# Expert loop of a routed vision tower: the second expert's gate and up projections moved one tile ahead, the row transposes moved to the end of the step

## The reference, cut to what matters

```
macro_scores = sigmoid(xf @ macro_w)                 # T x 4: one group of the four is chosen
micro_scores = sigmoid(einsum('td,gde->tge', xf, micro_w))
w = (macro_full[:, :, None] * micro_full).reshape(T, 8)
gate = silu(einsum('td,edf->tef', xf, gate_w))       # 256 -> 512
up = einsum('td,edf->tef', xf, up_w)                 # 256 -> 512
h = gate * up
out = einsum('te,tef,efd->td', w, h, down_w)         # 512 -> 256
```

## Time and profile before

| | |
|---|---|
| median of 3 runs | 2495.08 us (2494.74 to 2496.54) |
| the profiled execution | 2493.25 us, of which the profile's span is 2491.4 us |
| busy share of the span | PE 89%, DVE 74%, ACT 65%, POOL 47% |
| the expert loop | from 2288.3 us to the end of the span, about 203 us |

### The profile page before, as it was taken

One profiled execution on the slowest core, in us unless ns is written; L12 is line 12 of the kernel. 1 busy time (PEld: TensorE's weight loads), 2 busy tenths in 40 slices (PEclk: granted clock), 3 DMA queues, 4 the chain that ended last, 5 costly groups with the idle time before them and its releaser, 6 DMA issues.

```text
span 2491.4 us, 61244 instructions
## 1 busy us (share of the span) xinstructions
PE 2223.1 (89%) x19318; PEld 1660.7 (67%) x19318; DVE 1833.0 (74%) x5685; ACT 1607.2 (65%) x4899; POOL 1175.8 (47%) x2201
## 2 busy tenths in 40 slices
PE   0289999999989999999989999999899999988998
PEld 0257777777767777777667777777677777765655
DVE  8667777777767787777767777777678888886533
ACT  3257777776667777776667777777677777774322
POOL 1046555554556555555555555554566555541101
PEclk9889999999999999999999999999999999999999
DMA  3564444445554444444644444445543334345110
GB/s 118 140 172 116 106 107 112 113 129 155 132 158 123 111 109 111 106 123 144 180 118 114 113 110 113 121 135 146 158 106 97 94 100 109 99 136 187 54 46 23
DMA packets 378059, 295.35 MB, mean 119 GB/s; under 512 B 45087, under 2 KB 350721, under 8 KB 376739
## 3 DMA queue, kind: packets, MB, share of 16 engines
q1 hardware_dynamic: 370603, 272.41, 41.8%
q10 hardware_dynamic: 4864, 12.68, 1.5%
q0 software_dynamic: 2272, 6.35, 0.7%
HBM read 137.45 MB, written 72.07 MB: 84 GB/s over the span
## 4 chain that ended last, share of the span: by engine, by line
PE 33%; ACT 24%; DVE 12%; POOL 8%; SPq 7%; issue 6%; DMA 4%; DVEq 0%; POOLq 0%; ACTq 0%
ACT e_rows L2168 11%; PE bk L2066 5%; PE bk L2078 5%; SPq L1532 4%; PE bk L1272 4%; ACT p_flat L2150 4%; PE bk L2035 4%; PE bk L1906 3%; DVE x L2425 3%; DVE o_rows L2333 3%; ACT rel L2099 2%; POOL arena L1727 2%; PE bk L1894 2%; POOL arena L1725 2%; PE bk L1845 2%
## 5 line engine op out<-in xcount | busy, mean ns | idle before, releaser
L2168 ACT ACTIVATE e_rows<-e_rows,nb 128x257 f32<-128x257 f32 x1024 | 516.1, 515 | 34.9 <-DVE nb L2362 34.2
L2362 DVE CUSTOM_DVE_ANT_0 e_rows<-bk,arena 128x257 f32<-128x257 f32 x1024 | 390.1, 418 | 72.0 <-PE bk L1940 70.7
L1845 PE MATMUL bk<-hin,arena 128*128 128x257 f16 x3072 | 422.0, 274 | 16.7 <-DMA hin<-hd_dram 11.1
L2324 DVE TENSOR_TENSOR p_flat<-bk,p_flat 128x512 f16<-128x512 f32 x512 | 353.8, 691 | 66.7 <-ACT p_flat L2150 54.2
L1894 PE MATMUL bk<-ident,e_rows 128*128 128x128 f32 x2048 | 324.9, 281 | 51.8 <-ACT e_rows L2168 29.3
L1727 POOL TENSOR_TENSOR arena<-rel,arena 128x257 f16<-128x257 f32 x496 | 328.3, 662 | 41.4
L1845 PEld LDWEIGHTS bk<-hin,arena 128*128 128x128 f16 x3072 | 296.4, 97 | 67.4 <-issue 18.6
L1725 POOL TENSOR_SCALAR arena<-rel 128x257 f16<-128x257 f32 x496 | 203.7, 411 | 265.1 <-ACT rel L2099 258.4
L2150 ACT ACTIVATE p_flat<-bk 128x512 f16<-128x512 f32 x512 | 310.0, 605 | 7.9 <-PE bk L1894 7.9
L1894 PEld LDWEIGHTS bk<-ident,e_rows 128*128 128x128 f32 x2048 | 222.4, 141 | 136.9 <-ACT e_rows L2168 115.3
L1775 POOL TENSOR_SCALAR wf<-wf 128x256 f32<-128x256 f32 x216 | 94.1, 436 | 363.9 <-DMA wf<-in_w_dram 187.7
(11 more groups left out here) (327 smaller groups left out, 4232.8 us busy)
## 6 DMA issues: line engine op xcount, KB each, us to landing
arena<-arena SPq DMA_DIRECT2D x768, 128.5 KB, 3.5
wf<-in_w_dram SPq DMA_DIRECT2D x168, 128.0 KB, 2.8
w_split_dram<-wh SPq DMA_DIRECT2D x168, 128.0 KB, 2.4
xs_dram<-in_c_blank_dram SPq DMA_DIRECT2D x24, 772.5 KB
wf<-in_we_dram SPq DMA_DIRECT2D x96, 128.0 KB, 2.6
we_split_dram<-wh SPq DMA_DIRECT2D x96, 128.0 KB, 1.9
w_rest<-w_split_dram SPq DMA_DIRECT2D x12, 1024.0 KB, 17.2
arena<-we_split_dram SPq DMA_DIRECT2D x8, 1536.0 KB, 12.0
```

Of the source, the lines that this page charges most:

```text
L1845: r_ = mm(bank[4 + s % 2][:, 0:S], wcol(a, C_QKV, k, 3 * HD, chunk_at(s)), hin[:, m, k, :], start=i == 0, stop=i == 5)
L2168: act.activation(E[:, h % EB, qt, :], E[:, h % EB, qt, :], ACT.Exp, bias=nb[:, 2 * h + qt:2 * h + qt + 1], scale=-1.0, accum_out=sums[:, q ...
L2324: v.tensor_tensor(pt[:, h, 1, :, 0:IMG], bank[2 + h % 2][:, :].rearrange("p (k s) -> p k s", k=QT), pt[:, h, 0, :, 0:IMG], ALU.subtract).t ...
L2362: v.tensor_tensor_reduce(E[:, h % EB, qt, :], bank[qt][:, 0:S], cb[:, h, :], -SCORE, 3e38, ALU.add, ALU.min, nb[:, 2 * h + qt:2 * h + qt + ...
```

## The change

Only PE's list changes, in the loop over tiles. G(j+1,1), which stood at the start of step j+1, now stands in step j between D(j,0) and D(j,1), for all tiles but the first. R(j+2), which stood between D(j,0) and D(j,1), now stands behind D(j,1). The work is the same, instruction for instruction.

```
         for j in range(SLOT_TILES):
             g = self.group_of(pe, j)
-            self.gate_up(pe, j, 1, g)
             if j == 0:
+                self.gate_up(pe, 0, 1, g)
                 route_rank(pe, r, LAST - 1, self.side)
             transpose_inner(j, 0)
...
             down(j, 0, g)
             if j == 3:
                 transpose_image()
+            if j + 1 < SLOT_TILES:
+                self.gate_up(pe, j + 1, 1, self.group_of(pe, j + 1))
+            down(j, 1, g)
             if j + 2 < SLOT_TILES:
                 self.transpose_rows(pe, j + 2)
-            down(j, 1, g)
```

## The result

The changed kernel takes 2510.53 us (median of 4 runs, 2503.25 to 2512.81), the kernel before 2494.91 us beside it (4 runs, 2492.88 to 2496.54). The ratio is 1.0055, 95% interval 1.0039 to 1.0071: slower by about half a per cent, with the whole interval above 1. Run beside the kernel before once more (e1), the ratio was 1.0041 (1.0025 to 1.0057).

A forecast was written before the change was run, and what follows sets the result against it. TensorE, the busiest engine, bounds the kernel; its loop waits decide. New waits 24.6 less 12.9, less 0.3, plus 2.2 for the clock give 13.6 us more: 2508.6 us, range 2503.5 to 2511.5.

The forecast's parts named there:

- What the change takes away: Expert loop: waits for the low part of the inner product and R(9)'s for its load go, 12.9 us.
- The regular wait: Steps 6 and 8 to 18: G(j+1,0) waits 0.74 for `x_lo`, step 9.66 instead of 9.50; 8.9 us.
- The side steps: New waits: step 1 2.1, its end 1.8, step 3 3.3, step 4 1.8, step 5 3.9, step 7 2.8 us.
- TensorE's clock: Step 5, behind the 3.9 us wait: the granted clock falls to 0.50 once, costing 2.2 us.
- The price of a gap below 2 us: TensorE gaps below 2 us in the loop: clock cost taken as nothing.
- The load of tile 9: Load lands 4.91 us after the second list; R(9), now 3.9 us further back, no longer waits for it.
- The sum: New waits 24.6 less 12.9, 0.3 off at the end, plus clock 2.2: 13.6 us slower, 2508.6 us.
- third rival: Side steps' blocks are covered, regular steps alone remain, +0.8; 2496 to 2500 with half of the rest; chance 0.06.
- not slower: G(j+1,0) doesn't wait for its rows, `x_lo` coming within 0.69 of R's start; 2495.4 us or below; chance 0.04.
- the clock stays: Step 5's gap: the waits come but the clock does not fall; 2506.5 us; chance 0.27.
- falls more than once: Clock falls also in steps 3 to 5 or 7, 2.2 us per further fall; 2511 us; chance 0.08.
- side work costs less: Side steps' blocks are covered by something taken as fixed; 2496 to 2500 us; chance 0.06.

The follow-up runs named there:

- e5: Changed kernel with R(j+2) put back ahead of D(j,1), so D(j,0), G(j+1,1), R(j+2), D(j,1) in all steps; 2493.41 us, ratio 0.9990.
- e8: Kernel before up to step 6, from step 7 on the order D(j,0), G(j+1,1), R(j+2), D(j,1); 2487.56 us, ratio 0.9964.
- e6: Against the changed kernel, row transposes put back so only gate and up is moved: D(j,0), R(j+2), G(j+1,1), D(j,1); 2500.48 us, ratio 1.0016.
- e7: Against the kernel before, only the row transposes moved, R(j+2) behind D(j,1); 2497.81 us, ratio 1.0011.
- e2: Against the kernel before, the new order in steps 0 to 6 only; 2508.07 us, ratio 1.0041.
- e3: Against the kernel before, the new order from step 7 on only; 2496.58 us, ratio 0.9998.
- e4: Changed kernel plus twelve matmuls ahead of the ranks in step 5, whose results G(6,0) overwrites; 2506.48 us, ratio 1.0042.
- e10: Changed kernel with R(j+2) put back ahead of D(j,1), G(j+1,1) left moved, profiled again for the clock; loop time 192.4 us.
- e11: Changed kernel with the row transposes put back, only gate and up moved, profiled again for the clock; loop time 199.3 us.

## Why the prediction was right

The direction, the mechanism and most sizes held. Lengths of the steps, T(j,0) to T(j+1,0), against the prediction's waits:

| step | before | after | difference | predicted |
|---|---|---|---|---|
| 0 | 9.55 | 8.95 | -0.6 | -0.6 |
| 1 | 10.45 | 13.39 | +2.9 | +3.1 |
| 2 | 9.50 | 8.95 | -0.6 | -0.6 |
| 3 | 10.46 | 12.58 | +2.1 | +2.5 |
| 4 | 10.64 | 11.83 | +1.2 | +1.4 |
| 5 | 10.56 | 14.85 | +4.3 | +4.8, 2.2 of it the clock |
| 6 | 9.50 | 9.66 | +0.2 | +0.2 |
| 7 | 10.42 | 11.62 | +1.2 | +1.3 |
| 8 to 18 | 104.26 | 106.09 | +1.8 | +1.8 |
| behind T(19,0) | 10.86 | 10.68 | -0.2 | -0.3 |

The sum is 12.4 where the prediction had 13.6. (The predicted column takes the waits that the text names for a step, less those that the step had before.)

- *What the change takes away*: right. The low part of (j,1) is never waited for between D(j,0) and D(j,1), and R(9) not for its load.
- *The regular wait*: predicted 0.74 and 9.66 a step, measured 0.60 idle, 15 times, and 9.66. The exact agreement of the step is partly luck: the wait was 0.76 (2404.06 + 0.44 to 2405.26), and the work without waits 8.89 (e5, e8) and not 8.92, as R takes 0.22 when it need not wait. e6 and e7 show that the wait needs both moves, e5 that with G moved R's place decides.
- *The side steps*: each at or a little under what lengths of before, laid end to end, had given; the clock aside, the largest miss is 0.3, in step 3 (2.12 measured, 2.45 from the prediction's terms). That they make the loss is shown by e2 (11.2 of 12.4 without the late steps) and e3 (0.2 without the early ones).
- *TensorE's clock*: the fall came where it was expected; its size was 1.70 and not 2.2, because the clock was low for 3.4 us of work (2353.9 to 2357.3), while behind the earlier trace rows it was low for 4.6 us of it (2272.51 to 2277.1). This term of the sum was too dear by 0.5. e4 removes the fall, and G(6,0) alone makes 1.69 of the 1.83 that its loop is shorter. The advice of the Trainium skill that the prediction weighed (TensorE: Matmul & The Clock Gate, "Why this matters for your kernels"), to leave no idle gaps between bursts of matmuls, agrees with these runs: 0.50 behind the gap of 3.71, 1.00 where it is filled (e4).
- *The price of a gap below 2 us* was taken as nothing. For the gaps of the change (up to 1.6 idle beside the long one) that held. Between 2 and 3.7 us the prediction said nothing; e5 showed a fall at 2.42, which the expectation for that experiment lacked.
- *The load of tile 9*: 4.91 behind the list was a length of one execution, not a constant; in e2 it was 3.44. It didn't matter for the changed kernel, where R(9) comes later than either.
- *The sum*: 2493.25 + 13.6 + 1.83 is 2508.7, not 2508.6, and the third rival with half of the rest comes to 2501, not 2500. Neither moves the range or a chance.
- *The rivals*: "not slower" is out by the 15 waits; "the clock stays" and "falls more than once" by the windows, which show one fall; "side work costs less" by e2.

The median, 2510.5, lies 15.6 above its neighbour where the loop explains 12.4. In e1 the ratio was 1.0041, about 10.2 us. Both intervals contain 12.4 (a ratio of 1.0050). So that the median came within 1.9 of the forecast is in part luck: the loop's loss was 1.2 under the forecast, and the part ahead of the loop, on which the forecast said nothing, added some 3. In the first profile the loop began 2.3 earlier than in that of before, and the profiled execution was the fastest of its four. Why the part ahead of the loop, the same code in all these kernels, takes 2292.9 to 2303.0 in the profiles is open; nothing here was run on it.

## What to carry to other kernels

Moving a block on one in-order engine moves the cover of two waits: the one that it now hides, and the one that it used to hide. Here the gate and up block and D(j,1) had covered the 1.43 from the row transposes to the low part of the rows; count for every producer what is left between it and its consumer, and put a short producer early enough rather than last. Work that hangs behind such a producer on other engines (table loads, routing) starts 3.9 us of TensorE's work later and can cost more than the regular steps. So change the order only where no side work hangs on it: e8 does, and is 0.36% faster than the kernel before (interval 0.22% to 0.49%).

## What the runs showed of the hardware that was not expected

- A gap of 2.42 us idle on TensorE, between the four transposes T(5,0) and the small rank products, was followed by a granted clock of 0.50 in two of two executions (e5, e10), 0.2 to 0.3 us after work had begun again. A gap of 2.12 at the same place left it at 1.00 in two of two (e6, e11). The gaps of 1.1 to 1.6 idle elsewhere in the loop left it at 1.00. That the 0.3 us between 2.12 and 2.42 decide is not shown: the orders ahead of the gap differ too, and there are two executions of each.
- Behind one and the same gap of 3.71 the moment of the fall differed: 1.0 us after the first rank product in the changed kernel, 0.9 in e1, and 0.4 ahead of it in e2. The earlier it came, the less it cost: G(6,0) lost 1.70 in the changed kernel and 1.29 in e2.
- The loop times of the same kernel agree within 0.1 us (208.60 and 208.58; 192.46 and 192.37; 199.35 and 199.33), while the point at which the loop starts moves by about 10 us between profiles. For a change inside the loop, the loop time of one trace told more than the medians of whole times.
